# Householder tridiagonalisation: two row tiles of A x on TensorE, a new order of the step, and zero matmuls in the last block

## The reference, cut to what matters

```python
L = jnp.diag(deg) - A
L_norm = d_inv_sqrt[:, None] * L * d_inv_sqrt[None, :]
_, U = jnp.linalg.eigh(L_norm)
agg = jnp.einsum('mn,bnd->bmd', U.T, features)
```

## Time and profile before

| | |
|---|---|
| median of 3 runs | 4098.8 us (4097.18 to 4100.27) |
| profiled execution: its own time | 4102.27 us |
| profiled execution: span | 4100.2 us |
| TensorE clock granted, mean over the span | 0.858 |
| PE / PEld / DVE / ACT busy | 78% / 47% / 80% / 37% |
| from the first next-x (L487) to the last | 57.8 to 2097.4 us |

### The profile page before, as it was taken

The page is one execution under the profiler, slowest core; times in us unless marked ns, Lnnn a source line. Parts: engine busy times, 40 slices in busy tenths (PEclk is TensorE's granted clock), DMA queues, the critical chain, the costliest instruction groups (busy, mean ns, idle before and its releaser), DMA issues. The chain is left out here.

```text
span 4100.2 us, 61184 instructions
## 1 busy us (share of the span) xinstructions
PE 3204.2 (78%) x13932; PEld 1946.8 (47%) x14106; DVE 3297.1 (80%) x21659; ACT 1534.2 (37%) x5534; POOL 55.7 (1%) x71
## 2 busy tenths in 40 slices
PE   5888888888889999888877566555128899998859
PEld 3555555555555555677754222343014443454337
DVE  7999999999999999999989899999964323455467
ACT  2444444333333434333323322112113325554545
POOL 0000000000000000000000000000000000120000
PEclk8999999999999999855559788655569999999969
DMA  0000000000000000000000000000020000000001
GB/s 11 1 1 1 1 1 1 1 1 2 1 1 1 1 2 2 1 1 1 1 1 1 1 1 1 1 1 1 0 71 1 0 0 0 0 1 0 0 6 37
DMA packets 14157, 16.38 MB, mean 4 GB/s; under 512 B 571, under 2 KB 10214, under 8 KB 13798
## 3 DMA queue, kind: packets, MB, share of 16 engines
q1 hardware_dynamic: 13798, 12.48, 1.1%
HBM read 8.28 MB, written 4.19 MB: 3 GB/s over the span
## 5 line engine op out<-in xcount | busy, mean ns | idle before, releaser
L207 PE MATMUL ps<-zero_stream 128*128 128x512 bf16 x2168 | 650.6, 380 | 6.0
L305 ACT ACTIVATE refl<-ps,tiny 128x1 f32<-128x1 f32 x511 | 133.6, 261 | 435.7 <-PE ps L245 280.5
L207 PEld LDWEIGHTS ps<-zero_stream 128*128 128x128 bf16 x2324 | 252.1, 121 | 91.4 <-issue 31.6
L256 PEld LDWEIGHTS ps<-dot_parts,ones 128*128 128x128 f32 x766 | 114.5, 188 | 333.7 <-DVE dot_parts L434 332.8
L319 ACT ACTIVATE vectors<-WihT,refl 128x4 f32<-128x4 f32 (+2 forms) x383 | 115.0, 300 | 401.0 <-DVE refl L440 396.0
L256 PE MATMUL ps<-dot_parts,ones 128*128 128x2 f32 x766 | 146.2, 261 | 143.3 <-DVE dot_parts L434 140.6
L234 PE MATMUL ps<-ident,vectors 128*128 128x128 f32 x1148 | 207.1, 289 | 18.3 <-DVE vectors L487 1.3
L381 DVE CUSTOM_DVE_ANT_0 products<-ps,UT 128x511 f32<-128x511 f32 (+60 forms) x426 | 215.0, 533 | 6.8 <-PE ps L234 6.4
L234 PEld LDWEIGHTS ps<-ident,vectors 128*128 128x128 f32 x1148 | 115.1, 135 | 206.1 <-DVE vectors L487 205.6
L687 ACT ACTIVATE sturm_signs<-sturm_products,sign_bias 128x576 bf16<-128x576 f32 x96 | 74.4, 775 | 352.4 <-DVE products_mark L714 352.4
L1727 ACT ACTIVATE gates<-ps,gate_bias 128x512 f32<-128x512 f32 (+1 forms) x252 | 152.7, 637 | 130.9 <-PE ps L1714 95.9
(11 more groups left out here) (611 smaller groups left out, 8413.6 us busy)
## 6 DMA issues: line engine op xcount, KB each, us to landing
out_dram<-x SPq DMA_DIRECT2D x16, 256.0 KB, 2.3
adj<-in_adj_dram SPq DMA_DIRECT2D x1, 1024.0 KB, 5.3
l2w_in<-in_L_gnn_W_dram SPq DMA_DIRECT2D x2, 128.0 KB
Wqkv<-in_L_gnn_Wqkv_dram SPq DMA_DIRECT2D x1, 192.0 KB
L_gnn_W<-in_L_gnn_W_dram SPq DMA_DIRECT2D x2, 64.0 KB
L_gnn_Wg<-in_L_gnn_Wg_dram SPq DMA_DIRECT2D x2, 64.0 KB
x<-in_x_dram SPq DMA_DIRECT2D x4, 0.5 KB
L_gnn_Wo<-in_L_gnn_Wo_dram SPq DMA_DIRECT2D x1, 64.0 KB
```

The lines of the kernel that those rows point to most:

```text
L207: nc.tensor.matmul(MA[t][:],still[:,0:P],still[:],start=False,stop=True,skip_group_check=True)
L256: nc.tensor.matmul(dots(m),ones[:],dp[:],start=True,stop=True).then_inc(dot_ps,1)
L305: nc.scalar.activation(s[:,u,Y:Y+1],NG[:,0:1] if wide else NG[:,1:2],ACT.Sqrt,bias=tiny[:,0:1]).then_inc(root,1)
```

## The change

It does the following in `tridiagonalise`.

- PE computes two row tiles of A x (2 and 3) in blocks 0, 1 and 2, in every step; DVE multiplies tiles 0 and 1 in block 0, tile 1 in block 1, none in block 2. Block 2 therefore has no transposes of x, and its pair products and dots are matmuls over two tiles, as in block 3.
- The pairs are stored interleaved (b u, w in neighbouring columns). The row selected and the pair dots lie in one PSUM bank, and the two correction products become one instruction (`by_both`), which waits for both.
- The norm has its own matmul in every block, ahead of the products of A in blocks 0 and 1, behind the first one in block 2.
- x below the diagonal is made by ACT (two copies) and no longer by DVE.
- DVE's order: the share of the next x that comes from x (denominator, reciprocals, x/S, beta x/S) stands ahead of the last rows of y and the dot parts in blocks 0 and 1; in block 2 behind y; p comes last.
- ACT: b u and its half stand ahead of the copy of the updated tile; the pairs of a full panel are copied once more in turned order (`pairs_turned`), and the transposed rows are copied at the end of the panel's last step (two copies, not three at the start of the step after). tau and esub of a step are kept in the next one.
- Zero matmuls: 1 or 2 ahead of the dots and 2 at the end of the step in blocks 0 to 2; 2 or 3 and 2 in block 3, where the last two stand behind the selection of the next row.
- In block 3 the reflector is formed from a signed unit vector (`sh`) and twice the norm.
- Elsewhere: the last leaf of the factorisation adds PIVOT to its state (two DVE instructions in all).

The core of the diff:

```diff
 def pe_tiles(m):
-    b=m//P
-    if ends_panel(m) and m<=P or m>PANEL and m%PANEL==1 and b<NT-1: return range(0)
-    return range(NT-1,NT)
+    return range(NT-1 if regime(m)==3 else NT-2,NT)
 def streams(m):
+    if regime(m)==3: return (2 if update_tile(m) else 3,2)
+    return (1 if update_tile(m) or ends_panel(m) else 2,2)
...
+                def product(m, j, rows=None):
+                    b=m//P; o=(j-pe_tiles(m)[0])*WIDE
+                    pe.wait_ge(A_copied,copies_of(version(m)))
+                    if PANEL<m<P+PANEL: pe.wait_ge(gt_copied,2*((m-1)//PANEL))
+                    for t in range(NT-1,b-1,-1) if rows is None else rows:
+                        ins=nc.tensor.matmul(ax(m)[:,o:o+WIDE],A[version(m)%2][:,t,j*P:(j+1)*P],XG[:,t,X_:X_+1].broadcast_to([P,WIDE]),start=t==NT-1,stop=t==b)
+                    if j==pe_tiles(m)[0] and t==b: ins.then_inc(Ax_ps,1)
...
+                    if r<3:
+                        if r==2: product(m,NT-1)
+                        else:
...
+                        norm(m)
+                        if r==0: product(m,NT-1)
+                        if m>1: pe.wait_ge(ub_ready,m-1); pe.wait_ge(w_ready,m-1)
+                        if r==2: pair_products(m)
+                        row_selected(m,b)
+                        if r==0: pair_sums(m)
+                        if r==1:
+                            product(m,NT-1,range(NT-1,b,-1)); pair_sums(m); product(m,NT-1,range(b,b+1))
+                        product(m,NT-2)
+                        if ends_panel(m): transposed(m//PANEL-1)
+                        if update_tile(m): updated(*update_tile(m))
+                        streamed(m,streams(m)[0])
...
                     if TAIL<=m+1<N:
                         pe.wait_ge(ub_ready,m); pe.wait_ge(pc_ready,m)
+                        row_selected(m+1,NT-1)
+                    streamed(m,streams(m)[1])
...
                     def sign():
+                        if wide: v.wait_ge(*(g_ps,m-1) if L and r<2 else (sel_ps,m))
                     def shift():
-                        after("T2")
+                        v.wait_ge(t2_ready,m); v.wait_ge(h_ready,m)
+                    def by_both():
+                        v.wait_ge(*(sel_ps,m) if r==2 else (g_ps,m-1))
                     def x_by_shift():
-                        if m>1: v.wait_ge(xm_ready,m-1)
+                        v.wait_ge(xm_ready,m); v.wait_ge(u_ready,m)
...
+                    if r<2:
+                        pair_parts()
+                        v.wait_ge(A_copied,copies_of(version(m))); v.wait_ge(xrow_ps,m)
+                    if r==0:
+                        multiply(1); inverse(); multiply(1); sign(); by_both(); corrections(); reflector(); column_of_A()
+                        first_rows_of_y(); denominator(); inverses(); x_by_shift(); x_scaled(); last_rows_of_y(); dot_parts(); y_below(); y_scaled(); p_column()
+                    elif r==1:
+                        multiply(1); inverse(); twice_norm(); by_both(); sign(); shift(); corrections(); reflector(); column_of_A()
+                        first_rows_of_y(); denominator(); inverses(); x_by_shift(); x_scaled(); last_rows_of_y(); dot_parts(); y_below(); y_scaled(); p_column()
+                    elif r==2:
+                        inverse(); twice_norm(); by_both(); sign(); shift(); corrections(); reflector(); v.wait_ge(A_copied,copies_of(version(m))); column_of_A()
+                        last_rows_of_y(); denominator(); inverses(); x_by_shift(); x_scaled(); y_below(); y_scaled(); p_column()
+                    else:
+                        by_rows(); inverse(); sign(); twice_norm(); signed_unit(); by_dots(); reflector(); shift(); corrections()
+                        denominator(); column_of_A(); last_rows_of_y(); inverses(); y_below()
```

More of the change, by code:

```diff
@@ new lines, in norm, with pair_sums @@
+                def norm(m):
+                    pe.wait_ge(nrm_ready,m)
+                    if m>1: pe.wait_ge(kap_ready,m-1)
+                    nc.tensor.matmul(norm2(m),ones[:],gp[:,0:1],start=True,stop=True).then_inc(s2_ps,1)
+                def pair_sums(m):
+                    L=pending(m)
+                    if not L: return
+                    pe.wait_ge(gp_ready,m-1)
+                    nc.tensor.matmul(in_pairs(pair_dots(m)[:,2+2*L[0]:2+2*L[1]]),ones[:],swapped(gp[:,2+2*L[0]:2+2*L[1]]),start=True,stop=True).then_inc(g_ps,1)
@@ L249, in _ @@
[L249 to L256, removed]
@@ L257, in _ @@
-                        streamed(m,streams(m)[2])
+                        if r<2:
+                            pe.wait_ge(dp_ready,m)
+                            nc.tensor.matmul(dots(m),ones[:],dp[:],start=True,stop=True).then_inc(dot_ps,1)
+                        else:
+                            pe.wait_ge(y_ready,m)
+                            for t in range(b,NT):
+                                ins=nc.tensor.matmul(dots(m),V[:,t,m-1:m].broadcast_to([P,P]),XG[:,t,Y_:Y_+2],start=t==b,stop=t==NT-1)
+                            ins.then_inc(dot_ps,1)
@@ L340, in _ @@
                 v.wait_ge(x_ready,1)
-                link(nc.vector.tensor_tensor(xm[:],XG[:,:,X_],below[:,:,0],ALU.mult))
                 row_at=[0]
@@ L406, in corrections @@
-                    def corrections(last):
-                        if not L: return
-                        after(last)
-                        mark("cor",nc.vector.tensor_reduce(cor[:,:,sl],cprod[:,:,sl,0:2*n],AX.X,ALU.add))
-                    def reflector():
-                        if b>0: after("S")
-                        else: v.wait_ge(s_ready,m)
+                    def by_both():
+                        if not L: return
+                        v.wait_ge(*(sel_ps,m) if r==2 else (g_ps,m-1))
+                        both=psum[7][:,0:2*ROW0].rearrange("p (q c) -> p q c",c=ROW0)[:,:,2+2*L[0]:2+2*L[1]]
+                        mark("cp",nc.vector.tensor_tensor(cprod[:,:,sl,0:n2],pairs().unsqueeze(1).broadcast_to([P,2,NB,n2]),both.unsqueeze(2).broadcast_to([P,2,NB,n2]),ALU.mult))
@@ L475, in step @@
                     else:
                         v.wait_ge(ds,row_at[0])
-                        by_rows(); inverse(); sign(); twice_norm(); by_dots(); shift(); corrections("cy")
-                        reflector(); denominator(); column_of_A(); matrix_times_x()
-                        inverses(); y_below()
+                        by_rows(); inverse(); sign(); twice_norm(); signed_unit(); by_dots(); reflector(); shift(); corrections()
+                        denominator(); column_of_A(); last_rows_of_y(); inverses(); y_below()
@@ L485, in step @@
                     if m<LAST:
-                        v.wait_ge(dot_ps,m); after(last)
+                        v.wait_ge(dot_ps,m); v.wait_ge(ds,max(done["xt"],done["yq"]))
                         nc.vector.scalar_tensor_tensor(out=XG[:,sl,X_],in0=xt[:,sl],scalar=dots(m)[:,0:1],in1=yq[:,sl],op0=ALU.mult,op1=ALU.subtract).then_inc(x_ready,1)
@@ L1045, in _ @@
                                 if j==0: at[dr]=r.at()
+                        if j==NL-1 and u==LEAF-1:
+                            for dr in range(2):
+                                v.wait_ge(row,at[dr])
+                                r.inc(nc.vector.tensor_scalar(state[:,dr,0:w],state[:,dr,0:w],PIVOT,None,ALU.add))
+                                at[dr]=r.at()
                         if j or not first:
```

275 lines of the change are left out of this document (128 added, 147 removed).

## The result

The changed kernel takes 4252.5 us (median of 4 runs, 4251.7 to 4254.6) against 4098.6 for the kernel before on the same chip: a ratio of 1.0377, 95% interval 1.0364 to 1.0390. The change costs 154 us. Forecast were 4215, with a range of 4150 to 4260. L numbers from here on are lines of the kernel after; its next x is L505 (L487 before), its reflector L444 (L413), its root L325 (L305).

What follows compares the result with a forecast made beforehand. Bound: one loop from x to next x, along DVE. Blocks 0 to 3 add 10, 47, 52 and 7, +116 us; profiled 4102.3 makes 4218, which lies 3.5 above the median, so 4215 us; range 4150 to 4260.

Steps and rivals of the forecast that it cites:

- Block 1 and block 0, the order: Dependent instructions ahead of the dot parts lengthen reflector to next x, 1.37 to 1.97; block 1 +47 us, block 0 +10.
- the working: Block 1's step 197 worked out start by start on PE and DVE, from x to next x at 4.54 us.
- the forecast for the phases: Block 0: steps of 5.07 to 5.22 us as pairs grow; copies ahead of the root move to the panel's end.
- The four prices: Timeline costs: free DVE starts 0.07 or 0.13 apart, dependent start 0.04 after, late second wait 0.10, PE pass 0.112 us.
- the second wait: An instruction whose late wait is the second of two starts 0.10 us after it; at 0.04, blocks 1 and 2 lose 50 less.
- block 2, +52 forecast: Block 2: a step averages 4.00 us against 3.60 before, +52 us over 128 steps.
- Block 3, +7 forecast: Block 3: full clock, but two zero matmuls delay the norm; step 3.13 us against 3.07, +7 us.
- The rival by count of instructions: DVE's time goes by its instruction count, so the change is faster, about 3930 us; chance 0.08.
- more is late than I see: Rival: more is late (ACT's copies, reads in new patterns), giving 4245 to 4300 us; chance 0.13.
- the likeliest one: The case that all goes as worked out, 4185 to 4245 us; chance 0.55.

Runs made afterwards that it cites:

- fill: The kernel after, with DVE's order of before in blocks 0 to 2, nothing added or removed: 4060.9 us.
- before_x_ahead: The kernel before, with the new DVE order alone in blocks 0 to 2: 4325.7 us.
- swap: The kernel after, with the two waits ahead of shift and of x/S exchanged so the late semaphore is waited for first: 4202.4 us.
- combined_root: combined, with ACT no longer waiting for x ahead of its wait for the norm in block 3: 4016.7 us.
- combined: The kernel after, with the edits of fill, swap and b3_zeros_early together: 4028.8 us.
- onetile: The kernel after, with PE computing one row tile in blocks 0 and 1, as before, and DVE one more: 4590.0 us.
- b3_zeros_early: The kernel after, with all zero matmuls of block 3 ahead of the dots and none in front of the norm: 4241.1 us.

## Why the prediction was right, and where it was off

**Block 1 and block 0, the order.** Right, in mechanism and size. In step 197 every start of the working stands within 0.06 of the trace; next x comes at 4.52, worked out 4.54. `by_both` is fed by PE's queue as forecast, so the multiply that left DVE bought little there. The order itself was put at 0.60 a step (1.97 against 1.37 from reflector to next x) and measured 0.62; undoing it gave 0.53 and 0.49 in blocks 0 and 1, less than the 0.58 and 0.63 expected, since y then waits for PE there, and 0.43 in the undisturbed steps of block 2. fill and before_x_ahead show that the dependent run is the cause. In block 0 the forecast for the phases held too: phase 5, three steps ahead of the panel's end, went from 4.72 to 5.03 (5.07 worked out), phase 1 gained (5.76 to 5.54) as its copies moved away.

**The four prices.** swap and combined_root show the second wait, 0.10 against 0.03 or 0.04, on DVE and on ACT. The forecast put what it is worth at 50 us, 0.2 a step in blocks 1 and 2 alone; swap gained 50, with 0.15 and 0.14 a step there, 0.08 in block 0 and fewer falls of the clock in block 2 (2 steps for 27). That the two sums agree is luck: the forecast counted every second wait in two blocks, swap exchanged two a step in blocks 1 and 2 and one in block 0, and some of its gain is clock.

**The term mis-sized most: block 2, +52 forecast, +74 measured.** Two parts. The falls of the clock were not foreseen: 27 steps at 4.46 against 4.10 undisturbed, 10 us. Weight loads of four passes in such a step, and in an undisturbed one:

```profile
1589.61 1.06 PEld L229 LDWEIGHTS ps<-vectors,UT 128*128 128x128 f32 x4 [0.41 <-DVE vectors L505]
```

```profile
1556.96 0.52 PEld L229 LDWEIGHTS ps<-vectors,U 128*128 128x128 f32 x4 [0.89 <-DVE vectors L505]
```

A pass at half the clock takes double, and PE's queue is what `by_both` waits for. The other 12 us are the undisturbed step, 4.10 where 4.00 was worked out: starts slip by 0.01 to 0.06 each along the chain, reciprocals 2.98 for 2.95, y/S 3.72 for 3.65, next x 4.04 for 3.96 in a step with 5 pairs. About 2 us are in eight steps, phase 3 of every second panel, which take 4.42 where the same phase of the other panels takes 4.14: in step 267 the denominator starts 0.34 behind the last rows of y, in step 259 0.07. The same eight are longer in fill, swap and combined. No cause is shown.

**Block 3, +7 forecast, +25 measured.** Its mechanism held: clock near full, zeros in front of the norm, the norm's matmul right behind one. Missed was that ACT's wait for the norm had become its second, since `act.wait_ge(x_ready,m)` now stands in every block: 0.06 a step, 7 us by combined_root's median step. It was a wait that the diff adds and that the working did not list. The falls of the clock, 16 steps at 3.75 against 3.19, are 9 us more. The forecast took the full clock because PE would have as much to do per microsecond as in block 1; PE is busy 85% of block 3 (352 of 414.5 us) where it was 88% of block 1 before, and the clock stood at 0.95. The net result hides how it came about: at half the clock, without zeros, the block costs the same 414 us.

**The rival by count of instructions.** Dead: fill runs the same instructions 192 us faster than after. The Trainium skill (VectorE: DVE Perf Modes, "The DRAIN you can't avoid") says that in a run of eight copies a semaphore after each costs nothing extra, and ("Rules for kernel authors") that one should minimise operations and not semaphores. As a guide to this kernel's time that fails: fill and swap change neither the number of instructions nor that of semaphores and gain 192 and 50 us, and combined_root takes one wait of ACT away and gains 12.

The measured 4252.5 lies in the range but in the case "more is late than I see", given 0.13, not in the likeliest one. What was late was not what that case named (copies, new read patterns) but falls of the clock, one wait and small slips in block 2. That these came to some 38 us and stayed inside the range is in part luck, since none of them was priced.

**Open.** What sets a single fall of the clock in blocks 2 and 3. The same code of block 3 had 16 such steps in one run and 28 in another; the experiments change how many there are without showing what starts one. The small slips of block 2 stay unexplained too. Of the gain that remains without the order, no run tells the second tile, the moves to ACT and the single correction product apart; onetile prices only the tile.

## What to carry to other kernels

On an engine that passes short dependent instructions, put the work that the next engine waits for as early as its inputs allow, and lay the dependent run (here denominator, reciprocals, x/S) into the time in which the other engine works; moved ahead, it cost 0.5 us a step without one more instruction. Where an instruction waits for several semaphores, wait for the late one first, and look for waits that an edit adds in front of an old one on any engine. Work that keeps the clock up belongs where PE has to wait anyway (here ahead of the dots, while y is made), not where it is still running when the next input arrives: moved there, the zeros of block 3 took 0.14 off an undisturbed step, though not off the steps with a fall.

## What the runs showed of the hardware that was not expected

- One wait in front of a late wait costs 0.06 to 0.07 us a time, on DVE (x/S 0.10 to 0.03 after the reciprocals) and on ACT (root 0.10 to 0.04); over blocks 0 to 2 of the kernel after, exchanging the waits gave 1.2%. Where DVE then waits for another engine, as in block 1 of combined, it gives nothing.
- Less work for PE in a longer step cost more in clock than in itself. onetile made undisturbed steps 0.37 and 0.30 us longer, but the clock fell to 0.78 and 0.60 and blocks 0 and 1 took 148 and 173 us more; PE was busy 74% of block 0 there, 88% in the kernel after at clock 1.00.
- Falls are brief but dear in proportion: in block 3 of b3_zeros_early a step with one costs 4.27 us against 3.08, and their number differs from kernel to kernel in code that did not change.
